# Gram bursts, eleven looked-up features in all units, and the last two tiles' layers one by one, in a recommendation tower

## The reference

```python
e = jnp.stack([tbl_0[ids[:, 0]], tbl_1[ids[:, 1]],
...
dot_products = jnp.einsum('bnd,bmd->bnm', inputs, inputs)
r, c = np.tril_indices(num_feas, k=-1)
flat_interactions = dot_products[:, c, r]
...
h = jnp.concatenate([z, dense_ctx], axis=1)
h = jnp.maximum(h @ W_top1 + b_top1, 0.0)
h = jnp.maximum(h @ W_top2 + b_top2, 0.0)
y = h @ W_top3
```

## Time and profile before

| what | us |
|---|---|
| time, median of three runs | 503.46 |
| the three runs | 501.92, 503.46, 503.59 |
| span of the profiled execution | 358.7 |
| median less span | 144.8 |
| TensorE busy in the span | 333.7 (93%) |
| GpSimd busy in the span | 250.4 (70%) |
| VectorE busy in the span | 246.3 (69%) |
| ScalarE busy in the span | 144.4 (40%) |

### The profile page before, as it was taken

One profiled execution on the slowest core, in us unless ns is written; L12 is line 12 of the kernel. 1 busy time (PEld: TensorE's weight loads), 2 busy tenths in 40 slices (PEclk: granted clock), 3 DMA queues, 4 the chain that ended last, 5 costly groups with the idle time before them and its releaser, 6 DMA issues.

```text
span 358.7 us, 13616 instructions
## 1 busy us (share of the span) xinstructions
PE 333.7 (93%) x6094; PEld 303.4 (85%) x6094; DVE 246.3 (69%) x329; ACT 144.4 (40%) x265; POOL 250.4 (70%) x271
## 2 busy tenths in 40 slices
PE   1879699989999989999999999999999999999896
PEld 0779499978999979898889989999899989997775
DVE  3959979975488935878197965968387955961142
ACT  2536524444433433335343453435343353435320
POOL 5777777777777777777777777777777777777200
PEclk9969989999999999999999999999999999999999
DMA  6997744534333353443333452434533443322100
GB/s 184 306 318 196 205 136 107 102 93 91 83 93 82 90 99 75 96 96 80 93 88 82 115 85 77 105 84 81 102 89 83 99 98 74 84 55 55 27 3 1
DMA packets 26155, 36.86 MB, mean 103 GB/s; under 512 B 8451, under 2 KB 20099, under 8 KB 26098
## 3 DMA queue, kind: packets, MB, share of 16 engines
q0 software_dynamic: 8448, 17.32, 20.5%
q1 hardware_dynamic: 17506, 18.16, 20.1%
q10 hardware_dynamic: 144, 0.52, 0.4%
HBM read 35.97 MB, written 0.01 MB: 100 GB/s over the span
## 4 chain that ended last, share of the span: by engine, by line
PE 57%; POOL 26%; issue 10%; DVE 3%; DMA 3%; ACT 1%; DVEq 0%; ACTq 0%
POOL rows L450 26%; PE e_banks L482 25%; PE w_banks L543 9%; PE g_banks L513 8%; PE w_banks L554 7%; PE e_banks L494 6%; DMA rows<-in_tbl,idx 2%; DVE one_hot L672 2%; PE w_banks L532 1%; DVE zt L686 1%; DMA idx<-in_idx 1%; ACT et L340 0%; ACT h L333 0%; ACT et L350 0%; DVE a L720 0%
## 5 line engine op out<-in xcount | busy, mean ns | idle before, releaser
L450 POOL DMA_INDIRECT rows<-in_tbl,idx x264 | 249.6, 945 | 82.9 <-issue 78.0
L672 DVE TENSOR_TENSOR one_hot<-ids_wide,row_no 128x1024 fp32r<-128x1024 int32 x160 | 186.3, 1215 | 76.5 <-PE e_banks L482 72.5
L482 PE MATMUL e_banks<-one_hot,table_hi 128*128 128x256 f32 x672 | 172.2, 294 | 3.4 <-issue 3.4
L482 PE MATMUL e_banks<-one_hot,table_lo 128*128 128x256 f32 x672 | 167.0, 287 | 0.0
L482 PEld LDWEIGHTS e_banks<-one_hot,table_hi 128*128 128x128 f32 x672 | 131.4, 196 | 4.4 <-issue 4.2
L482 PEld LDWEIGHTS e_banks<-one_hot,table_lo 128*128 128x128 f32 x672 | 131.6, 196 | 0.2
L350 ACT ACTIVATE et<-e_banks 128x256 f32<-128x256 f32 x84 | 57.9, 689 | 89.3 <-PE e_banks L482 89.3
L340 ACT ACTIVATE et<-e_banks 128x512 f32<-128x512 f32 (+1 forms) x68 | 45.0, 664 | 52.3 <-PE e_banks L494 51.5
L513 PEld LDWEIGHTS g_banks<-et 128*26 128x26 f32 x4096 | 41.7, 103 | 17.7 <-issue 13.3
L513 PE MATMUL g_banks<-et 128*26 128x26 f32 x4096 | 50.0, 191 | 1.8 <-DVE zt L686 1.3
L494 PE MATMUL e_banks<-ident,rows 128*128 128x128 f32 x264 | 43.0, 285 | 5.5 <-DMA rows<-in_tbl,idx 5.5
(11 more groups left out here) (25 smaller groups left out, 67.7 us busy)
## 6 DMA issues: line engine op xcount, KB each, us to landing
ids_wide<-in_ids SPq DMA_DIRECT2D x80, 128.0 KB
et<-in_kept_tables SPq DMA_DIRECT2D x10, 512.0 KB, 10.1
rows<-in_tbl,idx POOLq DMA_INDIRECT x264
et<-in_kept_tables ACTq DMA_DIRECT2D x1, 512.0 KB, 3.9
a1T<-in_ids SPq DMA_DIRECT2D x4, 128.0 KB, 10.8
w<-in_w SPq DMA_DIRECT2D x2, 256.0 KB
w<-in_W_top SPq DMA_DIRECT2D x1, 512.0 KB
w<-in_w SPq DMA_DIRECT2D x1, 222.0 KB
```

Of the source, the lines that this page charges most:

```text
L450: pool.indirect_dma_start(rows[:, k % RING, a, :], None, tables[f], bass.IndirectOffsetOnAxis(ap=idx[:, t, f:f + 1], axis=0)).then_inc(row ...
L482: last = nc.tensor.matmul(e_bank[n % E_BANKS][:, 0:UNIT], part[:, q, c, :], one_hot[:, hot_slot(o, piece), c % PIECE, :], start=(c == 0 an ...
L672: nc.vector.tensor_tensor(one_hot[:, hot_slot(o, piece), :, :], ids_place(o).unsqueeze(1).broadcast_to([P, PIECE, UNIT]), row_no[:, piece ...
```

## The change

Four things change in the list of steps, and the code that runs them follows.

- `GATHERED_IN` is empty: all units look up eleven features. There are 88 look-ups and not 84, 256 gathers and not 264, and 64 ticks and not 68. The host hands over three tables less as arrays of their own.
- A tile's eight pieces of grams stand in one tick, one behind the other, and not two in each of four ticks.
- Within a tick the three H steps alternate with look-ups. Layer 2 of a unit stands one tick later. The costs in `COLUMNS` are others.
- The last unit's tiles pass the layers one by one: H1 and M1 are H and L1 for one tile. Tile 14's stand ahead of tile 15's grams. Where the last unit's drains alternated between ScalarE and VectorE, now those of tile 15 do.

```diff
-GATHERED_IN = {0: 3, 4: 1}
+GATHERED_IN = {}
...
-        at = 1 + (n - AHEAD) * 7 // 10
-        step = [("OH", 0, q)] + [("HI", n + AHEAD)]
+        at = 1 + (n - AHEAD) * 6 // 10
+        step = [("OH", 0, q)] + [("HI", m) for m in range(n + AHEAD, min(n + AHEAD + 1, NOH))]
...
         at = TILE_AT[t + 1] + (t == 0)
-        for p in range(G_PIECES):
-            step = [("G", t, p)] + ([("turn", t), ("pack", t)] if p == G_PIECES - 1 else [])
-            grams[at + p * 4 // G_PIECES].append(step)
-    for u in range(LAST):
-        at, then = TILE_AT[PAIR * (u + 1) + 1], TILE_AT[min(PAIR * (u + 2), LAST_TILE)]
+        grams[at] += [("G", t, p) for p in range(G_PIECES)] + [("turn", t), ("pack", t)]
+    for u in range(LAST - 1):
+        at, then = TILE_AT[PAIR * (u + 1) + 1], TILE_AT[PAIR * (u + 2)]
...
-        if u < LAST - 1:
-            layers[then].append([("L2", u, 0)])
-            layers[then + 1].append([("L2", u, 1)])
-
-    COLUMNS = {"T": 1024, "OH": 4096, "G": 1024, "H": 1024, "L1": 3072, "L2": 4096}
...
+        layers[then + 1].append([("L2", u, 0)])
+        layers[then + 2].append([("L2", u, 1)])
+
+    at, tile = TILE_AT[LAST_TILE], LAST_TILE - 1
+    turns[at] += [[("H", LAST - 1, c)] for c in range(KC)]
+    layers[at + 1] += [[("L1", LAST - 1, m)] for m in range(M1)]
+    layers[at + 2] += [[("L2", LAST - 1, j)] for j in range(PAIR)] + [[("H1", tile, c)] for c in range(KC)]
+    layers[at + 2] += [[("M1", tile, m)] for m in range(M1)]
+    layers[at + 3].append([("L2", LAST, 0)])
+
+    COLUMNS = {"T": 1024, "OH": 4608, "G": 704, "H": 640, "L1": 3072, "L2": 4096, "H1": 320, "M1": 1536}
...
+    END = [("G", LAST_TILE, p) for p in range(G_PIECES)] + [("turn", LAST_TILE), ("pack", LAST_TILE)] \
+        + [("H1", LAST_TILE, c) for c in range(KC)] + [("M1", LAST_TILE, m) for m in range(M1)] \
+        + [("L2", LAST, PAIR - 1)]
...
-        for step in look_ups[k] + layers[k]:
-            STEPS += step
-        for turn, piece in itertools.zip_longest(turns[k], grams[k], fillvalue=[]):
-            STEPS += turn + piece
+        for turn, step in itertools.zip_longest(turns[k], look_ups[k] + layers[k], fillvalue=[]):
+            STEPS += turn + step
+        STEPS += grams[k]
...
-            return "dve" if s[1] == LAST and s[2] % 2 == 1 else "act"
+            return "dve" if s[1] == LAST_TILE and s[0] in ("H1", "M1") and s[2] % 2 == 1 else "act"
...
+            def turn_tile_pairs(s):
+                _, t, c = s
+                n = W_AT[s]
+                free_w_bank(n)
+                wait_packed(t, c)
+                nc.tensor.transpose(w_bank[n % WB][0:KROWS[c], 0:P], h[:, t % PAIR, c * P:c * P + KROWS[c]], ident[:]
+                                    ).then_inc(w_filled, 1)
+
+            def layer1_tile(s):
+                _, t, m = s
+                n = W_AT[s]
+                free_w_bank(n)
+                for c in range(KC):
+                    if m == 0:
+                        w_emptied(W_AT["H1", t, c])
+                    last = nc.tensor.matmul(w_bank[n % WB][:, 0:P], w1[0:KROWS[c], c, m * P:(m + 1) * P],
+                                            hT[0:KROWS[c], c, t % PAIR, :],
+                                            start=(c == 0), stop=(c == KC - 1))
+                last.then_inc(w_filled, 1)
```

More of the change, by code:

```diff
@@ L150, in dlrm_tower @@
         layers[at + 2] += [[("L1", u, 2)], [("L1", u, 3)]]
-        if u < LAST - 1:
-            layers[then].append([("L2", u, 0)])
-            layers[then + 1].append([("L2", u, 1)])
-    COLUMNS = {"T": 1024, "OH": 4096, "G": 1024, "H": 1024, "L1": 3072, "L2": 4096}
-    LOOK_UPS_FROM = [0, TILE_AT[1] + 1] + [TILE_AT[PAIR * (u - 1)] + 4 for u in range(2, UNITS + 1)]
-    load = [sum(COLUMNS[step[0][0]] for step in turns[k] + layers[k] + grams[k]) for k in range(TICKS)]
+        layers[then + 1].append([("L2", u, 0)])
[7 more added lines that the diff above has]
+    COLUMNS = {"T": 1024, "OH": 4608, "G": 704, "H": 640, "L1": 3072, "L2": 4096, "H1": 320, "M1": 1536}
+    LOOK_UPS_FROM = [0, TILE_AT[1] + 2] + [TILE_AT[PAIR * (u - 1)] + 4 for u in range(2, UNITS + 1)]
+    load = [COLUMNS["T"] + sum(COLUMNS[step[0]] for part in turns[k] + layers[k] + [grams[k][:G_PIECES]] for step in part)
+            for k in range(TICKS)]
     for u in range(1, UNITS):
@@ L166, in dlrm_tower @@
             look_ups[k][i] = [("OH", u, q)]
-    pieces = [("G", LAST_TILE, p) for p in range(G_PIECES)]
-    END = pieces[:G_PIECES // 2] + [("L2", LAST - 1, 0)] + pieces[G_PIECES // 2:] \
-        + [("turn", LAST_TILE), ("pack", LAST_TILE), ("L2", LAST - 1, 1)] \
-        + [("H", LAST, c) for c in range(KC)] + [("L1", LAST, m) for m in range(M1)] \
-        + [("L2", LAST, j) for j in range(PAIR)]
+    END = [("G", LAST_TILE, p) for p in range(G_PIECES)] + [("turn", LAST_TILE), ("pack", LAST_TILE)] \
+        + [("H1", LAST_TILE, c) for c in range(KC)] + [("M1", LAST_TILE, m) for m in range(M1)] \
+        + [("L2", LAST, PAIR - 1)]
     STEPS = list(FIRST)
@@ L612, in drain_turned @@
                 act.wait_ge(w_filled, n + 1)
-                cols = w_bank[n % WB][:, 0:UNIT].rearrange("p (j b) -> p j b", b=P)
-                copy("act", hT[0:KROWS[c], c, :, :], cols[0:KROWS[c]]).then_inc(w_drained[n % WB], 1)
+                cols, tiles = turned_cols(s)
+                copy("act", hT[0:KROWS[c], c, tiles, :], cols[0:KROWS[c]]).then_inc(w_drained[n % WB], 1)
             def drain_layer1(s):
@@ L645, in _ @@
                     pack_first(s[1])
-                elif s[0] == "H" and w_engine(s) == "act":
+                elif s[0] in ("H", "H1") and w_engine(s) == "act":
                     drain_turned(s)
-                elif s[0] == "L1" and w_engine(s) == "act":
+                elif s[0] in ("L1", "M1") and w_engine(s) == "act":
                     drain_layer1(s)
@@ L749, in _ @@
                     pack_rest(s[1])
-                elif s[0] == "H" and w_engine(s) == "dve":
+                elif s[0] in ("H", "H1") and w_engine(s) == "dve":
                     drain_turned(s)
-                elif s[0] == "L1" and w_engine(s) == "dve":
+                elif s[0] in ("L1", "M1") and w_engine(s) == "dve":
                     drain_layer1(s)
```

32 lines of the change are left out of this document (24 added, 8 removed).

## The result

The changed kernel takes 518.75 us (median of four runs, 517.89 to 519.62), the kernel before 503.37 (501.92 to 503.59): a ratio of 1.0345, with an interval of 1.031 to 1.038. It is slower by 3.4%. Forecast were 498.3 us, within 492 to 505, and with 0.68 that it would be faster.

A forecast was written before the change was run, and what follows sets the result against it. The prediction took TensorE and GpSimd's gathers as level bounds. It summed 320.0 us to tile 15's first chunk and 33.5 to the end into a 353.5 us span, plus 144.8 around it: 498.3 us, range 492 to 505.

The forecast's parts named there:

- 503.46 - 358.7 = 144.8 lies around it, and nothing in the change touches that: Outside the profiled span: 144.8 us of the kernel's time, taken as unchanged and added to the forecast span.
- the sum: Whole span, added up in four stages: 353.5 us after the change, 5.2 less than 358.7.
- What a burst may lose is a wait inside it: TensorE's gram bursts of eight pieces: one wait of 0.30 us per burst, bounds 0 and 1.0.
- 0.42 for the pieces and 2 x 0.09 for the switches: Gram phases of a tile: eight pieces together save 0.42 us, and each avoided switch from look-up to grams saves 0.09.
- starved bursts: Rival, chance 0.15: each burst half costs what 341.88 cost, 16 x 0.7 = 11.2 us more, 509.5 us.
- So TensorE and GpSimd are level: Whole kernel: TensorE's work and GpSimd's unbroken gathers, 4.31 to 333.08 us, share the span; shortening one alone gives little.
- Stages (a) to (c): Start to tile 15: first grams at 50.0 us, tile 3's first chunk at 79.4, tile 15's at 320.0.
- The look-ups' price: TensorE: four added look-ups of two tiles each, 1.96 us per tile, cost +7.8 us.
- the ten gather microseconds: GpSimd: 8 gathers fewer at 1.248 us save 10.0 us, so the last gather issues at 323.1.
- Passing the two tiles one by one gains next to nothing by itself: Tile 15's first chunk to the end: 33.5 us against 33.3 before, bounds 31.0 and 38.
- The clock: Rival, chance 0.10: TensorE at the lower clock for ten microseconds behind the first burst loses 5 us, whole 503.
- signs of being wrong: Changed profile: issue waits over 10 us; clock under 1 at 40-60 us; one-hot waits after unit 1; units under 39.5 us.

The follow-up runs named there:

- the kernel with plain copies: The kernel before with each of the 264 gathers replaced by a plain transfer of its table's first 128 rows: 353.33 us, ratio 0.7053.
- fours: The kernel before with four gram pieces in each of two ticks and plain transfers of the first 128 rows for the gathers: 347.83 us, ratio 0.6951.
- eights: The kernel before with a tile's eight gram pieces in one burst and plain transfers of the first 128 rows for the gathers: 401.4 us, ratio 0.7977.
- the spread version of the changed kernel: The changed kernel with its grams of tiles 0 to 13 spread over four ticks again, two pieces each: ratio 1.0039 to the kernel before.
- the second profile of the kernel before: The kernel before, unchanged, run and profiled again: 507.97 us, span 505.7 us, ratio 1.0008.
- tidy addresses: The kernel before with indirect gathers indexed by partition number, so that they bring the first 128 rows of each table: ratio 1.0033.
- half the gathers: The kernel before with every second gather of a chunk replaced by a plain transfer of the first 128 rows: 362.76 us, ratio 0.7238.

## Why the prediction was wrong

Two steps failed. One put the time of the kernel in the wrong place; the other gave the change the wrong sign.

**"503.46 - 358.7 = 144.8 lies around it, and nothing in the change touches that".** Around the span lie 1.8 us; the profiled execution was not one of the timed kind. Its gram line (50.0 | 1.8) and its span (358.7) are within 5% and 2% of those of the kernel without indirect gathers (47.7 | 2.4, 351.9), so it looks like this program when the gathers don't hold TensorE up, and the sum described that. The 144.8 us were inside the kernel, two thirds of them (93.6 us of 147.0) as idle time of TensorE: 73.4 us ahead of grams, nearly all of it without a releaser in the profile, and 21.8 at the start. The 13.3 us of "issue" waits ahead of gram weights that the prediction read from the earlier trace rows are no trace of it, since the kernel with plain copies has 14.0 of them. The two numbers could have told: 29% of the time lay outside the span, and I named nothing that it could be spent on.

**"What a burst may lose is a wait inside it", taken as 0.30, bounds 0 and 1.0.** This term turned the sign. The mechanism was right, the size too small by eight: 2.5 us a burst with plain copies (37.5 / 15), 2.34 and 2.37 in the last two bursts of the changed kernel. It would have failed the sum with the right span too: in the state that the sum described, with plain copies, the whole change costs 410.9 - 353.3 = 57.6 us, where the sum had a gain of 5.2. My bounds came from four pieces in a row, and fours behave unlike eights: they gained 5.5 us, eights lost 48.1. The gain of gathering phases is there for fours, but smaller than the prediction's terms: 0.42 for the pieces and 2 x 0.09 for the switches make 0.60 a tile, 9.0 us for 15 tiles, and 5.5 was measured. Of the rivals, starved bursts had the right sign and place and was priced at 0.7 more a burst instead of 2.2. The Trainium skill, "Runtime: NRT & Kernel Launch", section "Instruction fetch mechanics", lets blocks of 256 instructions be fetched ahead and calls a crossing mostly hidden; here a burst of eight (256 rows of matmul and 256 of weight loads) holds a wait that is not hidden, a burst of four does not. The measurement decides.

**"So TensorE and GpSimd are level", gathers back to back to 333.08.** In the timed executions GpSimd is ahead and waits for TensorE (132.1 us before, 114.7 after). Stages (a) to (c), 50.0, 79.4 and 320.0, came out at 82.41 for the first grams, 127.35 for tile 3 and 474.33 for tile 15. (The pitch of the gathers in the earlier trace rows is 328.77 / 263 = 1.250 us, not 1.248; nothing hangs on it.)

**The gathers and look-ups.** The look-ups' price was right where it can be seen: +7.8 forecast, +7.9 measured with plain copies. With real gathers the pair of edits gains 1.6% and does not cost. GpSimd's own time, for which I counted the ten gather microseconds, can't be the reason, as GpSimd waits for TensorE; that fewer gathers hold TensorE up less is likely, and not shown.

**Bursts with real gathers.** They cost 2.5% alone, 3.0% by the spread version of the changed kernel. There the grams' own lines fall (148.4 to 108.8 us) and the loss reappears at the steps behind them, where TensorE waits for ScalarE's drains. By stages, against the second profile of the kernel before (from another job, span 505.7): tile 3 begins 4.4 us earlier (127.35 against 131.71), a unit takes 57.8 and not 56.8 us, and from tile 15's first chunk to the end it is 41.8 and not 33.0. So of the 14.8 us lost between these two profiles, 8.7 are at the end.

**"Passing the two tiles one by one gains next to nothing by itself", 33.5 us.** It loses. The stage took 41.8, 8.3 more than forecast. The two bursts account for 5.0 + 4.9 - 2 x 2.68 = 4.5 us of this, tile 15's layer 1 for 5.2 - 2.8 = 2.4 through the clock, the rest is spread over small steps. "The clock" was a rival of mine, but for the first ten microseconds, not for the end. Tile 14's layer 1 took 2.84 us against the 2.8 that I took: the step was sized rightly. With its bursts split the end still takes 36.7, 3.7 more than before, and its last layer 1 runs at 0.61.

Two of the prediction's signs of being wrong came: "issue" waits over 10 us (65.9), and a granted clock under 1 between 40 and 60 us (slices of 0.6 and 0.8 in the changed kernel's row).

**What stays open** is why indirect gathers hold the other engines up. Shown is that the indirect form does it in every timed execution (1.003 with tidy addresses, 0.705 with plain copies), that it stops with the last gather, that it is far from proportional (half the gathers leave 6% of it), and that neither a pause of 0.33 us after each gather nor a bound of four under way removes it. The density of gathers can't be all of it: in the execution of the earlier trace rows 264 of them ran back to back, 1.250 us apart, with TensorE at 93%. What made that execution different could not be found from its trace, and a version that reaches 350 us with all gathers was not found.

## What to carry to other kernels

Put the profiled span beside the time before anything else: where they differ by more than a few microseconds, profile again, since the page may show an execution whose waits are not those that are timed. "Issue" waits and waits for something "remote" on a single-core kernel are a cost of their own, and moving work can move them from one line to another, so judge an edit by the whole time. Long runs of tiny matmuls are worth breaking: here 128 rows of them at a stretch were free and 256 held a wait of 2.5 us.

## What the runs showed of the hardware

- Indirect gathers from GpSimd slow the other engines by much more than their bytes: 503 us against 353 with plain copies of the same size, in every execution that was timed; the one execution of the earlier trace rows had them at a span of 358.7. The granted clock goes with it: 9 tenths and over in 39 of 40 slices with plain copies (its PEclk row above), and in 17 of 40 of the changed kernel.
- The wait in a burst of eight has a place of its own. Counted over the built program, with two instructions a row of matmul and the waits between them, the instruction behind the wait was number 194 or 195 of a block of 256 for all 16 waits in the fifteen bursts with plain copies, though it fell after 154 rows in one and elsewhere in others, and for all 13 waits of over 1.5 us in the bursts of the changed kernel. The instruction queue makes 49 transfers of 16 KB in the changed kernel, and TensorE's 12622 instructions, counted the same way, are 49.3 blocks of 256. One of them fell into the burst of tile 14 (DMA view of 476.4 to 481.5 us: queue, packets, MB, share):

```profile
q8 instruction: 1, 0.02, 1.5%
```

  It began at 477.84 us and none began during the wait itself (478.2 to 480.54), so the wait ended 2.7 us after the transfer's start; the 16 waits with plain copies ended 2.2 to 2.9 us after one. All this points to the fetching of instructions in blocks. It is argued from place and time; what is shown is that the length of the burst decides.
- With gathers issued back to back from the start, TensorE stands still for 21.8 to 22.9 us behind its second chunk, and the clock is at 0.50:

```profile
22.00:44.00 22.00, 0.00 (x0) 0.00 (x0) 1.83 (x2) 0.61 (x2) 13.24 (x15) 0.53 0.40 114
```

  That row is the changed kernel's: one operation of VectorE, and the starts of one more and of two of ScalarE from 43.39 us on, while GpSimd issues 15 gathers. A pause of 0.33 us after each gather removes it. Without the pause it ends when GpSimd stops: in the unchanged kernel (GpSimd, and ScalarE last)

```profile
36.88 0.94 POOL L450 DMA_INDIRECT rows<-in_tbl,idx  x1 [0.30 <-issue]
42.79 0.94 POOL L450 DMA_INDIRECT rows<-in_tbl,idx  x1 [4.96 <-remote]
...
42.45 0.68 ACT L350 ACTIVATE et<-e_banks 128x256 f32<-128x256 f32 x1 [23.80 <-remote]
```

  the gather at 36.88 us is the 27th, which fills the ring of seven chunks, and 4.6 us after its end ScalarE, VectorE, GpSimd and TensorE all go on within a microsecond. The changed kernel does the same 4.5 us after its 28th. That the end of the unbroken run of gathers is what frees them was not tested.
